# Summing the scan states by transposes accumulated in PSUM, with part of the outer products on GpSimd

## The reference

```python
u = silu(conv1d(x_in) + conv_b)                  # 1024 channels
dt = softplus(dt_r @ dt_proj_w.T + dt_proj_b)
A = -exp(A_log)                                  # 1024 x 16 states
def step(h, inp):
    dA = exp(dt_t[:, :, None] * A)
    h = h * dA + (dt_t * u_t)[:, :, None] * B_t[:, None, :]
    y = einsum('bdn,bn->bd', h, C_t)             # the sum over the states
    return (h, y)
y = (ys + u * D_param) * silu(z)
out = y @ out_proj_w.T
```

## Time and profile before

| | us |
|---|---|
| median of 3 runs | 2406.55 (2406.52 to 2406.91) |
| span of the profiled execution | 2405.4 |
| main stage, first to last scan | 68.8 to 1911.8 |
| TensorE busy | 2232.3 (93%) |
| VectorE busy | 2163.1 (90%) |
| ScalarE busy | 1679.7 (70%) |
| GpSimd busy | 1908.1 (79%) |
| mean granted TensorE clock | 0.984 |

### The profile page before, as it was taken

The page is one execution under the profiler, slowest core; times in us unless marked ns, Lnnn a source line. Parts: engine busy times, 40 slices in busy tenths (PEclk is TensorE's granted clock), DMA queues, the critical chain, the costliest instruction groups (busy, mean ns, idle before and its releaser), DMA issues. The chain is left out here.

```text
span 2405.4 us, 24262 instructions
## 1 busy us (share of the span) xinstructions
PE 2232.3 (93%) x6966; PEld 1153.2 (48%) x6966; DVE 2163.1 (90%) x2363; ACT 1679.7 (70%) x3268; POOL 1908.1 (79%) x1244
## 2 busy tenths in 40 slices
PE   9899999989998999899989988998987999999999
PEld 3233434334433443344334333433333488988888
DVE  4899999999999999999999999999999966666666
ACT  3688777877787778778877887787555445466655
POOL 0699999999999999999999999999987822232225
PEclk9899999999999999999999999999998999999999
DMA  6610231041104110411051123103100121011113
GB/s 225 229 44 27 100 103 40 27 148 59 35 27 158 47 37 22 167 56 59 19 179 40 31 71 130 33 27 130 64 31 12 74 77 34 26 56 58 49 53 123
DMA packets 78050, 176.10 MB, mean 73 GB/s; under 512 B 7453, under 2 KB 10781, under 8 KB 77918
## 3 DMA queue, kind: packets, MB, share of 16 engines
q1 hardware_dynamic: 77918, 174.56, 21.6%
HBM read 157.23 MB, written 17.30 MB: 73 GB/s over the span
## 5 line engine op out<-in xcount | busy, mean ns | idle before, releaser
L1402 POOL TENSOR_TENSOR arena<-arena 128x1024 f32<-128x1024 f32 x512 | 1199.2, 2360 | 107.1 <-ACT arena L580 77.3
L1001 DVE TENSOR_TENSOR_SCAN arena<-ps,arena 128x512 f32<-128x512 f32 x1024 | 1241.7, 1256 | 1.3 <-ACT ps L580 1.2
L580 ACT ACTIVATE ps<-arena 128x512 f32<-128x512 f32 x1087 | 722.8, 681 | 367.2 <-DVE arena L1001 307.0
L318 PE MATMUL ps<-arena,keep 128*128 128x512 f32 x1782 | 863.3, 615 | 108.2 <-POOL arena L1402 74.9
L989 DVE TENSOR_TENSOR arena<-ps,arena 128x1024 f32<-128x1024 f32 x512 | 618.4, 1208 | 13.8 <-PE ps L318 11.1
L318 PEld LDWEIGHTS ps<-arena,keep 128*128 128x128 f32 x1782 | 333.6, 194 | 592.2 <-issue 338.4
L264 PE MATMUL ps<-arena 128*128 128x512 f32 x1024 | 459.9, 593 | 1.6 <-issue 0.8
L264 PEld LDWEIGHTS ps<-arena 128*128 128x128 f32 x1024 | 193.5, 190 | 248.8 <-issue 247.8
L580 ACT ACTIVATE arena<-arena 128x2 f32<-128x2 f32 (+2 forms) x599 | 228.4, 384 | 52.1 <-POOL arena L1347 17.1
L304 PE MATMUL ps<-arena 128*128 128x512 f32 x512 | 231.1, 592 | 0.0
L1359 POOL TENSOR_TENSOR arena<-arena 128x512 f32<-128x512 f32 x168 | 213.9, 1273 | 10.9 <-ACT arena L580 3.8
(11 more groups left out here) (146 smaller groups left out, 2701.7 us busy)
## 6 DMA issues: line engine op xcount, KB each, us to landing
arena<-scr_bc SPq DMA_DIRECT2D x128, 512.0 KB, 6.4
arena<-in_inT SPq DMA_DIRECT2D x128, 256.0 KB, 2.6
arena<-in_x SPq DMA_DIRECT2D x17, 512.0 KB, 4.3
scr_x<-arena SPq DMA_DIRECT2D x32, 256.0 KB, 2.2
arena_b<-scr_x SPq DMA_DIRECT2D x16, 512.0 KB, 3.8
arena_c<-scr_x SPq DMA_DIRECT2D x32, 256.0 KB, 2.9
out<-arena_c SPq DMA_DIRECT2D x32, 256.0 KB, 2.0
arena<-in_x SPq DMA_DIRECT2D x30, 256.0 KB, 3.3
```

What stands on the lines that cost most here:

```text
L318: last = e.matmul(YP, ident, hb[G % R][:, i, :], start=False, stop=(g == NG - 1 and i == n - 1))
L580: return e.activation(o_, i_, f, **kw)
L1001: e.tensor_tensor_scan(H, DA[s % 4], H, h0, MUL, ADD).then_inc(v_sc)
L1402: m_ = e.tensor_tensor(H, H, Ct[:, GN * g:GN * g + GN, :], MUL)
```

## The change

The sum over the states changes its operands. The states become the stationary operand, the identity the moving one, with the transpose flag: `nsum` issues eight 128 x 128 transposes for each group, accumulated in `YP`, which then holds the transposed sum of the unit. When it is complete ScalarE copies it to a new SBUF tile `yt` (step 5 of the next unit), and TensorE transposes it back (`y_back`, step 7) into a `BG` bank in which D*u has been put first. `y_fin` moves to step 8 and reads that bank. There are no pair sums any more (`halved`, `HALF`, `HALF0` and line 1407 go). `sz` has three buffers in place of four, which makes room for `yt`.

GpSimd makes the outer products of the groups that `pooled` picks, from `spt` in SBUF and not from `DU`, at step 2G - 6 of its own program. The short description of the change says 76; the condition in the diff picks 64. The scans of these groups, `load_B` and the softplus that overwrites `spt` wait for `g_ex`; the waits that counted VectorE's products count with `tt_no`.

`bank` now takes the step at which each use ends and gives out the bank that is free earlier. At the change of layer `y_back(63)` stands behind `q_mm(0)`, the last `out_mm` behind `v_mm(0)`, `y_copy(63)` between two splits on ScalarE and `y_fin(63)` behind two splits on VectorE. Some DMA semaphores are shared (`D0` is the count that they start from).

```diff
-        dt, xr, spt, xdbl[1], xs, sz = [sb(T) for _ in range(2)], [sb(512) for _ in range(2)], sb(T), sb(T), sb(2, 512), sb(4, T)
+        dt, xr, spt, xdbl[1], xs, sz = [sb(T) for _ in range(2)], [sb(512) for _ in range(2)], sb(T), sb(T), sb(2, 512), sb(3, T)
+        yt = sb(4, 128)
...
-        AT = {"dt": 4, "soft": 7, "add": 6, "du": 7, "copy": 12, "yf": 6, "proj": (6, 14), "xdbl": (7, 3)}
+        AT = {"dt": 4, "soft": 7, "add": 6, "du": 7, "copy": 12, "yt": 5, "yb": 7, "yf": 8, "proj": (6, 14), "xdbl": (7, 3)}
...
-        HALF = {0: (1, 2, 5, 6), 1: (2, 3, 6, 7), 2: (1, 2, 3, 6), 3: (0,), 4: (), 5: (), 6: (5,), 7: (0, 3, 4, 5, 7)}
...
-        HALF0 = {0: (1, 2, 3), 1: (5,), 2: (), 3: (4,), 4: (), 5: (), 6: (), 7: ()}
-        halved = lambda U, g: g in (HALF0 if U < 8 else HALF)[U % 8] and U != 39
+        pooled = lambda U, g: g in (1, 3) and U > 6 and U != 39 and (U % 8 in (0, 1, 2, 7) or U >= 56)
+        POOLED = [G for G in range(NU * NG) if pooled(*divmod(G, NG))]
+        ex_no = lambda G: sum(1 for g in POOLED if g < G)
+        tt_no = lambda G: G - ex_no(G)
+        EXP = {(2 * G - 6): G for G in POOLED}
...
-            def bank(key, release):
-                i = turn[0] = 1 - turn[0]
+            def bank(key, release, end=None):
+                i = 1 - turn[0] if end is None or until[0] == until[1] else int(until[1] < until[0])
+                turn[0], until[i] = i, -1 if end is None else end
...
             def nsum(G):
                 U, g = divmod(G, NG)
+                e.wait_ge(g_w, G + 1)
+                if g == 0:
+                    e.wait_ge(a_yt, U)
+                for i in range(GN):
+                    for q in range(4):
+                        last = e.matmul(YP[:, 128 * q:128 * q + 128], hb[G % R][:, i, 128 * q:128 * q + 128], ident,
+                                        start=(g == 0 and i == 0 and q == 0), stop=(g == NG - 1 and i == GN - 1 and q == 3), is_transpose=True)
+                last.then_inc(p_y)
+
+            def y_back(U, P):
                 c, j = divmod(U, 8)
-                if g == 0:
-                    e.wait_ge(a_dg, U + 1)
-                    e.wait_ge(a_su, su_of(c))
-                    e.wait_ge(v_yf, U)
-                    e.matmul(YP, dg[U % 2], u[c % 2][:, j, :], start=True, stop=False)
-                e.wait_ge(g_w, G + 1)
-                n = 1 if halved(U, g) else GN
-                for i in range(n):
-                    last = e.matmul(YP, ident, hb[G % R][:, i, :], start=False, stop=(g == NG - 1 and i == n - 1))
-                last.then_inc(p_y)
-
+                e.wait_ge(a_dg, U + 1)
+                e.wait_ge(a_su, su_of(c))
+                if U == NU - 1:
+                    e.wait_ge(a_yt, NU)
+                e.matmul(P, dg[U % 2], u[c % 2][:, j, :], start=True, stop=False)
+                e.wait_ge(a_yt, U + 1)
+                for q in range(4):
+                    last = e.matmul(P[:, 128 * q:128 * q + 128], yt[:, q, :], ident, start=False, stop=(q == 3), is_transpose=True)
+                last.then_inc(p_yb)
...
+                    if U > 0 and pr == AT["yb"]:
+                        y_back(U - 1, bank(("yb", U - 1), (v_yf, U), 16 * U + AT["yf"] + 0.6))
...
                 q_mm(2 * n)
                 if n == 0:
+                    y_back(NU - 1, YP)
+                v_mm(2 * n)
+                if n == 0:
                     for m in range(4):
                         out_mm(NCH - 1, m, 7, tail_P[m])
-                v_mm(2 * n)
...
                     e.wait_ge(a_du, U - 1)
+                    if ex_no(NG * U):
+                        e.wait_ge(g_ex, ex_no(NG * U))
...
+            def y_copy(U):
+                e.wait_ge(p_y, NG * U + NG)
+                if U:
+                    e.wait_ge(p_yb, U)
+                act(flat(yt), YP, ACT.Identity).then_inc(a_yt)
...
+                if U > 0 and pr == AT["yt"]:
+                    y_copy(U - 1)
...
             e.wait_ge(g_w, NG * NU)
-            for h in range(2):
-                split_raw(h, "v", h)
+            split_raw(0, "v", 0)
+            y_copy(NU - 1)
+            split_raw(1, "v", 1)
...
                 e.wait_ge(a_da, s + 1)
-                e.wait_ge(v_tt, s // 2 + 1)
+                if s // 2 in POOLED:
+                    e.wait_ge(g_ex, ex_no(s // 2 + 1))
+                else:
+                    e.wait_ge(v_tt, tt_no(s // 2 + 1))
...
-                e.wait_ge(p_y, NG * U + NG)
+                P = YP if U == NU - 1 else BG[bank_of["yb", U]]
+                e.wait_ge(p_yb, U + 1)
                 e.wait_ge(a_sz, U + 1)
-                e.tensor_tensor(u[c % 2][:, j, :], YP, sz[:, U % 4, :], MUL).then_inc(v_yf)
+                e.tensor_tensor(u[c % 2][:, j, :], P, sz[:, U % 3, :], MUL).then_inc(v_yf)
...
-                if pr % 2 == 0 and s // 2 + 1 < NG * NU:
+                if pr % 2 == 0 and s // 2 + 1 < NG * NU and s // 2 + 1 not in POOLED:
                     expand(s // 2 + 1)
...
-            y_fin(NU - 1)
             split_raw(0, "v", 0)
             split_raw(1, "v", 1)
+            y_fin(NU - 1)
...
+            def expand(G):
+                U, g = divmod(G, NG)
+                e.wait_ge(g_du, U)
+                if U % 8 == 0:
+                    e.wait_ge(d_B[g], 16 * (U // 8 + 1))
+                e.wait_ge(p_y, G - R + 1)
+                e.tensor_tensor(hb[G % R], spt.unsqueeze(1).broadcast_to([128, GN, T]), Bt[:, GN * g:GN * g + GN, :],
+                                MUL).then_inc(g_ex)
...
+                if s in EXP:
+                    expand(EXP[s])
...
-                    m_ = e.tensor_tensor(H, H, Ct[:, GN * g:GN * g + GN, :], MUL)
-                    if halved(U, g):
-                        halves += 1
-                        m_.then_inc(g_m)
-                        e.wait_ge(g_m, halves)
-                        m_ = e.tensor_tensor(H[:, 0, :], H[:, 0, :], H[:, 1, :], ADD)
-                    m_.then_inc(g_w)
+                    e.tensor_tensor(H, H, Ct[:, GN * g:GN * g + GN, :], MUL).then_inc(g_w)
...
                 if c:
-                    e.wait_ge(v_tt, NG * (8 * c - 1) + g + 1)
+                    G = NG * (8 * c - 1) + g
+                    e.wait_ge(*((g_ex, ex_no(G + 1)) if G in POOLED else (v_tt, tt_no(G + 1))))
```

More of the change, by code:

```diff
@@ L125, in program @@
         d_M = [sem(f"d_M{i}") for i in range(2)]
-        d_xo = [sem(f"d_xo{i}") for i in range(4)]
-        d_out = [sem(f"d_out{i}") for i in range(4)]
+        d_xo, d_out, D0 = d_B[0:4], d_C[0:4], 16 * NCH
         p_cond, p_col, p_gb, p_tr, p_w, p_xp, p_dt, p_y, p_op = (sem("p_" + n) for n in
             ("cond", "col", "gb", "tr", "w", "xp", "dt", "y", "op"))
+        p_yb, a_yt, g_ex = sem("p_yb"), sem("a_yt"), sem("g_ex")
         p_ft, p_q, p_v, p_k, p_qt, p_kt, p_kv, p_ya, p_o = (sem("p_" + n) for n in
@@ L213, in program @@
         tail_of = lambda U, pr: ([TAILM[U, pr]] if (U, pr) in TAILM else []) + TAILX.get((U, pr), [])
+        XEV_AT, OUT_AT = ({i: 16 * k[0] + k[1] for k, i in D.items()} for D in (XEV, OUTA))
+        NEV_AT = {2 * (U // 8 + 1) + i: 16 * U + pr for (U, pr), i in NEV.items()}
+        ZS_AT = {U + d: 16 * U + pr for U in range(NU) for (j, pr), ds in ZSILU.items() if U % 8 == j for d in ds}
+        ZS_AT.update({0: ZS0, 1: ZS0})
         su_of = lambda c: 5 + 3 * c
@@ L381, in _ @@
                             e.wait_ge(g_gw, 4 if c < 5 else 8)
-                            out_P = bank(("out", c - 1, n), (a_x1, 4 * (c - 1) + n + 1))
+                            out_P = bank(("out", c - 1, n), (a_x1, 4 * (c - 1) + n + 1), 128 * c + OUT_AT[n] + 0.6)
                             e.wait_ge(d_xr[n % 2], 16 * ((4 * (c - 1) + n) // 2 + 1))
@@ L422, in _ @@
             held8 = [(v_x1, 4), (v_sc, NS), (v_sc, NS), (v_sc, NS), (v_yf, NU), (v_x1, 3), (v_x1, 2), (v_x1, 2)]
-            order, nxt = list(range(8)), [1]
+            order, nxt, early = list(range(8)), [4], [1, 2, 3, 1]
             def bank8(key, release):
-                i = order[nxt[0] % len(order)]
-                nxt[0] += 1
+                if early:
+                    i = early.pop(0)
+                else:
+                    i = order[nxt[0] % len(order)]
+                    nxt[0] += 1
                 if held8[i] is not None:
@@ L695, in du_copy @@
                 e.wait_ge(g_du, U)
-                e.wait_ge(v_tt, NG * U)
+                e.wait_ge(v_tt, tt_no(NG * U))
                 act(DU, spt, ACT.Identity).then_inc(a_du)
@@ L700, in z_silu @@
                 e.wait_ge(p_w, z_no(U) + 1)
-                if U >= 4:
-                    e.wait_ge(v_yf, U - 3)
-                act(sz[:, U % 4, :], BG[bank_of["z", U]], ACT.Silu).then_inc(a_sz)
+                if U >= 3:
+                    e.wait_ge(v_yf, U - 2)
+                act(sz[:, U % 3, :], BG[bank_of["z", U]], ACT.Silu).then_inc(a_sz)
             def diag_D(U):
                 if U >= 2:
-                    e.wait_ge(p_y, NG * (U - 2) + 1)
```

(9 more changed lines are left out.)

29 lines of the change are left out of this document (15 added, 14 removed).

## The result

| | before | after |
|---|---|---|
| median, us | 2406.73 (2406.52 to 2408.14) | 2517.02 (2507.2 to 2523.11) |
| span of the profiled execution | 2405.4 | 2513.8 |
| mean granted TensorE clock | 0.984 | 0.910 |
| VectorE busy | 2163.1 (90%) | 2097.6 (83%) |
| last product of the last unit starts | 1921.26 | 2028.42 |

The changed kernel is slower: ratio 1.0453, interval 1.043 to 1.0476. The forecast was 2344.

A forecast was written before the change was run, and what follows sets the result against it. VectorE bounds ordinary chunks, with GpSimd a few us behind, and GpSimd bounds chunk 4. Gains 35.5 + 5.0 + 17.0 + 7.2 - 2.5 = 62.2 us; 2405.4 - 62.2 + 1.15 = 2344.4, say 2344, range 2322 to 2386.

The forecast's parts named there:

- `y_fin`'s path: Unit's end: last sum lands 12.2 us behind the last scan, `y_fin` about 14, so covered in middle chunks with little left.
- Its slower rival: ScalarE in `y_copy` holds up the exponentials if the last sum lands beyond 13.7 us: +95, 2439; chance 0.08.
- The gain of the products: Main stage: 64 outer products at 1.12 us leave VectorE, 71.7 us, the most the edit itself can bring, plus vanishing waits.
- one of them would fill the chunk: Ordinary chunks: GpSimd's 220.9 us plus 1.4 of waiting sets 222.3, a gain of 7.1 each, 35.5 for five.
- The product on GpSimd: GpSimd's outer product was taken to last 2.36 us, like line 1374's multiplication, and to cost 2.32 in a run.
- `y_copy` costs nothing by its work: ScalarE's 64 copies out of PSUM at 0.59 us, 4.7 us per chunk on 179 busy of 229, cost nothing.
- TensorE's relief: Sums by transposes in place of matmuls: 93.7 us of a chunk becomes 59.2, relief of 34 of its 210.
- the third rival: TensorE's clock falls to 1.2 GHz between projections, cold bursts cost more: 5 us per chunk, +35, 2379; chance 0.12.
- The change of layer: Between the two layers: +3.6 us later, normalization about 1 us earlier, taken together as a loss of 2.5 us.
- the +3.6 taken for the `out_mm` path: Change of layer: `out_mm` comes 4.0 us later by `y_back` and 12 matmuls, delaying the second mask's load; +3.6 seen.
- the 1 us to be gained by the missing pair sum: Change of layer: without the last pair sum the normalization starts about 1 us earlier.
- the 62.2 us forecast: Whole kernel's gain: 35.5 ordinary chunks, 5.0 chunk 4, 17.0 chunk 7, 7.2 chunk 0, less 2.5; chance 0.52.

The follow-up runs named there:

- 7: Changed kernel with `y_back` at step 9 in place of 7 and `y_fin` at step 11 in place of 8, nothing else: 2425.54 us.
- 5: Changed kernel with `y_back` writing into `YP` itself at step 4, no `BG` bank, `y_fin` at step 7, next unit's first sum waiting for it: 2429.18 us.
- 4: Changed kernel with the next unit's first sum put behind `y_back` on TensorE: 2483.83 us.
- experiment 8: Changed kernel with `y_back` at step 9, `y_fin` at 12, and the output projection's first bursts moved to steps 10 and 12: 2406.6 us, ratio 1.0001 to the kernel before.
- experiment 1: Changed kernel without products on GpSimd (`pooled` always false), transposes kept, no pair sums: 2520.41 us.
- 9: Kernel of 7 (`y_back` at step 9, `y_fin` at 11) with all products on VectorE, none on GpSimd: 2434.4 us.
- 6: Kernel of 5 (`y_back` into `YP`) with all products on VectorE, none on GpSimd: 2448.5 us.
- 12: Kernel of experiment 8 with all products on VectorE, none on GpSimd: 2447.02 us.
- 3: Changed kernel with each group's eight 128-column transposes issued as plain fp32 matmuls against the identity, transposes back kept: 2559.3 us.
- 10: Kernel of 7 with two bf16 matmuls of zeros added into `YP` amid every group's transposes: 2449.21 us.
- experiment 11: Kernel of experiment 8 with four z projection bursts moved by one or two steps: 2394.76 us, ratio 0.995 to the kernel before.

## Why the prediction was wrong

**The failed step: `y_fin`'s path.** The prediction worked out when the last sum lands and whether `y_copy` holds up the exponentials, then let `y_fin` at "step 8, about 14 us" stand as covered, "and the wait for the sum is rather shorter". Between the copy and `y_fin` it counted no `y_back` at all: not its own 1.3 us (3.0 in the first example; with it the forecast's own numbers give 12.2 + 0.6 + 1.3 = 14.1 us, no longer covered by 14), not the `BG` bank that it must be given at step 7, one step in which the bank of the projection to dt is held until the softplus of that same step has read it, and not the two things queued ahead of it on TensorE. In its place the runs showed 181.0 us of waits. The last sum was early, 7.5 us behind the last scan (median) and not 12.2; from there to the start of `y_back` went 5.0 us, up to 9.9. Moving `y_back` and `y_fin` by two and three steps took 91.5 us away with nothing else changed (7); another bank 88 (5); the order on TensorE alone 33 (4). These overlap and are not to be added, and how the 181 us divide between the bank, the queue and `y_fin`'s place stays open.

**Its slower rival** was ScalarE in `y_copy` with the exponentials behind it, 2439. The direction and the place (a unit's end, a few us in each unit) were near, the mechanism was not: scans wait 15.4 us in all in the changed kernel, half of it for GpSimd. Its condition, a last sum later than 13.7 us, was never met (11.5 at most). In experiment 8 the scans do wait 33.8 us for ScalarE; traced back to what ScalarE had last stood for, 6.4 of them lie behind the wait of `y_copy` for the last sum and 14.9 behind waits for projections.

**The gain of the products** was 71.7 us off VectorE: that this leaves VectorE and GpSimd busy for 219.1 and 217.6 us of a chunk (220.9 with GpSimd's gaps) was right within 2 us (219.5, 219.4). Not right was that one of them would fill the chunk. It is not the balance of the two that makes the waits into time: in experiment 1 VectorE has all the products and the loss is about the same. The same products brought 3.4 to 40 us (1 and the change, 9, 6, 12).

**The costs.** The product on GpSimd took 2360 ns, as line 1374 said. Eight transposes took 1.04 us at the full clock and 1.97 at the low one, as in the earlier trace rows. That `y_copy` costs nothing by its work held: ScalarE's waits for scans are 352.6 us. TensorE's relief, 34 us for each chunk, came out at 209.1 - 192.6 = 16.5, as part of the work runs at the lower clock: over the whole kernel the projections (line 272) are busy for 512.8 us in place of 459.9, transposes 597 in place of 512 x 0.87 = 445.

**The clock** fell as the third rival had it: 0.50 in stretches with transposes and little else, 0.910 on the mean; plain matmuls of the same shape kept it at 0.99 (3). By the rule of the Trainium skill (TensorE: Matmul & The Clock Gate, Part 4: PE-mode transpose), that transposes do not count as activity as matmuls do, this is what should come, and the traces agree with it: in the changed kernel 5 us at 0.50 with TensorE busy for 4.64, mostly with transposes, were followed by 5 us at 0.50 (570 to 580), while before, 5 us at 0.50 with 4.75 busy, with plain matmuls, were followed by 0.95. In experiment 3 alone the kind of instruction and the busy time change together. Its price there, 35 us, stays open: the bursts of 5.35 us lie on the way of the last sum in the first example, but both runs that raised the clock (3 and 10) put more work on TensorE, and with the clock still at 0.93 experiment 11 is below the kernel before.

**The change of layer** came out 1 us longer than forecast: the mask's load is issued 22.6 us behind the last scan's end in place of 19.1, +3.5. That is the +3.6 taken for the `out_mm` path; the 1 us to be gained by the missing pair sum is not seen in it.

**What it comes to.** Of the 62.2 us forecast, the terms on VectorE's and GpSimd's busy time hold, and the waits of VectorE, taken as nearly unchanged, grew by 170. The best order found gains 12.5 us. Whether a still better one reaches the 2344 was not tried.

## What to carry to other kernels

A result that takes one more hop (copy out, back in, out again) has to be costed as a whole path, with the step of the program at which each hop stands, what is queued ahead of it there, and who holds the buffer it needs at that step, not only the work of each hop. An offloaded product is worth what the order lets through, here 3 to 40 us of the same 72. Before such a change is given up, shift the consumer so that it asks later: two constants were worth 91 us here.

## What the runs showed of the hardware

fp32 transposes of 128 x 128 accumulate in a PSUM bank, 64 of them for a unit, started once and stopped once. Their price follows the granted clock: 8 in 1.04 us at 1.00, in 1.97 at 0.50. With them in place of the sum's matmuls the mean clock fell from 0.984 to 0.910; as plain matmuls, twice the records and more busy time, it was 0.988; two bf16 matmuls in each group brought 0.915 to 0.968. A 128 x 1024 product takes 2.36 us on GpSimd with both operands whole and with one broadcast, and 1.20 on VectorE with one operand in PSUM (1.12 from start to start).
